# Probabilities turned one period later, beside the new scores, in a fused gated attention and FFN block

## The reference

```python
# x, ctx: (32, 64, 512); H, HKV, DK = 32, 8, 128
Q = (layernorm(x) @ Wq.T).reshape(b, s, 8, 4, 128)
K = (ctx @ Wk.T).reshape(b, s, 8, 128)
V = (ctx @ Wv.T).reshape(b, s, 8, 128)
scores = einsum('bqhed,bkhd->bheqk', Q, K) * 128 ** -0.5     # causal
attn = einsum('bheqk,bkhd->bqhed', softmax(scores), V)
x = x + tanh(g_xattn) * (attn @ Wd.T)
...
x = x + tanh(g_ffn) * down(silu(gate(layernorm(x))) * up(layernorm(x)))
# gate, up, down: weights w * (su @ sv), inner size 1792
```

## Time and the profile before

| | us |
|---|---|
| median of 3 runs | 1472.08 (1470.79 to 1472.47) |
| the profiled execution | 1472.51 |
| its span, first to last instruction | 1470.7 |
| TensorE matmuls busy | 1451.0 (99%) |
| VectorE busy | 1070.5 (73%) |
| GpSimd busy | 820.2 (56%) |
| ScalarE busy | 642.4 (44%) |
| TensorE idle before a matmul, the longest of them in attention | 1.1 |

### The profile page before, as it was taken

The page is one execution under the profiler, slowest core; times in us unless marked ns, Lnnn a source line. Parts: engine busy times, 40 slices in busy tenths (PEclk is TensorE's granted clock), DMA queues, the critical chain, the costliest instruction groups (busy, mean ns, idle before and its releaser), DMA issues.

```text
span 1470.7 us, 20673 instructions
## 1 busy us (share of the span) xinstructions
PE 1451.0 (99%) x7322; PEld 1185.7 (81%) x7322; DVE 1070.5 (73%) x1578; ACT 642.4 (44%) x1118; POOL 820.2 (56%) x727
## 2 busy tenths in 40 slices
PE   8999999999999999999999999999999999999998
PEld 8878788888888777777777777887888888888887
DVE  5366677877677777767777778777488878767676
ACT  5355454554444343343433444443444444333343
POOL 5598899998888212111111332233388877666664
PEclk9999999999999999999999999999999999999999
DMA  8476677778987644333433334332011121311112
GB/s 274 150 229 210 221 253 250 260 232 291 361 268 265 229 142 140 115 115 134 139 115 115 115 124 155 138 137 65 22 59 50 43 61 48 122 43 59 49 55 75
DMA packets 116070, 218.02 MB, mean 148 GB/s; under 512 B 9472, under 2 KB 47616, under 8 KB 113920
## 3 DMA queue, kind: packets, MB, share of 16 engines
q1 hardware_dynamic: 115968, 216.70, 44.0%
HBM read 151.13 MB, written 65.54 MB: 147 GB/s over the span
## 4 chain that ended last, share of the span: by engine, by line
PE 90%; DVE 5%; issue 1%; DMA 1%; POOL 1%; ACT 1%; SPq 0%; DVEq 0%; ACTq 0%; POOLq 0%
PE bank L543 66%; PE bank L709 4%; PE bank L662 4%; PE bank L845 3%; PE bank L844 3%; PE bank L846 3%; PE bank L671 2%; PE bank L689 2%; DVE el L1265 1%; PE bank L587 1%; DMA c_raw<-in_ctx_t 1%; DVE er L1265 1%; PE bank L742 1%; DVE xc L1259 0%; DMA w_raw<-in_w 0%
## 5 line engine op out<-in xcount | busy, mean ns | idle before, releaser
L1601 POOL TENSOR_TENSOR wd_lo<-wd_raw,wd_hi 128x512 fp32r<-128x512 f32 x64 | 81.9, 1302 | 370.6 <-ACT wd_hi L1011 370.6
L543 PE MATMUL bank<-xc,wa_hi 128*128 128x512 f32 x896 | 277.3, 391 | 0.0
L543 PE MATMUL bank<-wd_hi,o_hi 128*128 128x512 f32 x512 | 202.4, 395 | 0.0
L543 PE MATMUL bank<-wd_hi,o_lo 128*128 128x512 f32 x512 | 199.9, 390 | 0.0
L543 PE MATMUL bank<-wd_lo,o_hi 128*128 128x512 f32 x512 | 199.5, 390 | 0.0
L543 PEld LDWEIGHTS bank<-xc,wa_hi 128*128 128x128 f32 x896 | 167.8, 188 | 35.9 <-issue 1.1
L543 PE MATMUL bank<-xc,wa_lo 128*128 128x512 f32 x448 | 174.5, 390 | 0.0
L1352 DVE TENSOR_TENSOR o_lo<-bank,o_hi 128x512 fp32r<-128x512 f32 x128 | 82.0, 682 | 100.2 <-ACT o_hi L1042 100.2
L1429 DVE SCALAR_TENSOR_TENSOR X<-bank,tg,X 128x512 f32<-128x512 f32 x221 | 154.4, 741 | 0.0
L543 PE MATMUL bank<-x_hi,wf_hi 128*128 128x512 f32 x392 | 153.1, 391 | 0.0
L543 PE MATMUL bank<-x_hi,wf_lo 128*128 128x512 f32 x392 | 152.5, 389 | 0.0
(11 more groups left out here) (180 smaller groups left out, 3411.1 us busy)
## 6 DMA issues: line engine op xcount, KB each, us to landing
q_scratch<-q_st SPq DMA_DIRECT2D x32, 1024.0 KB, 4.3
q_sb<-q_scratch SPq DMA_DIRECT2D x64, 512.0 KB, 5.7
w_raw<-in_wq SPq DMA_DIRECT2D x32, 512.0 KB, 4.0
wd_raw<-in_wd SPq DMA_DIRECT2D x16, 1024.0 KB, 5.1
f_raw<-ffn_eff_scratch SPq DMA_DIRECT2D x28, 512.0 KB, 3.6
er_raw<-in_sf_r SPq DMA_DIRECT2D x42, 256.0 KB, 4.0
e_raw<-in_wf SPq DMA_DIRECT2D x42, 256.0 KB, 5.3
ffn_eff_scratch<-e_eff SPq DMA_DIRECT2D x42, 256.0 KB, 5.1
```

Of the source, the lines that this page charges most:

```text
L543: last = pe.matmul(to, a, b, start=(start and n == 0), stop=(stop and n == 3 * len(pairs) - 1), skip_group_check=onto)
L1601: g.tensor_tensor(wd_lo[h % 2][:, e, :], wd_raw[:, e, :], f32(wd_hi[h % 2][:, e, :]), ALU.subtract).then_inc(g_wd, 1)
```

## The change

TensorE's period becomes: scores of u and u+1, probability transpositions of u-2 and u-1, score transpositions of u and u+1, weighted values of u-2 and u-1, outputs. `prob` has four buffers instead of two. ScalarE copies the new scores before the turned probabilities, and splits output weights before `out_hi(u-1)`. VectorE takes `masked_minus_max(u)` before `out_lo(u-2)`, and one addition to X goes between the two normalisations. At the entry, unit 0's probabilities are turned in bank 4 and output (0, 1) goes to bank 4. At the exit, the last pair's probabilities are turned within the FFN's first step.

```diff
-    prob = [at(15, "prob0", [P, CB * G // 2, S]), at(203, "prob1", [P, CB * G // 2, S])]
+    prob = [at(kib, f"prob{n}", [P, CB * G // 2, S]) for n, kib in enumerate((15, 203, 199, 201))]
@@ output_bank(u, t) @@
-            return 6 if t else 1
+            return (6 if u else 4) if t else 1
...
     def prob_bank(u):
-        return 7 if u == 0 else 2 + u % 2
+        return 4 if u == 0 else 2 + u % 2
@@ TensorE, scores(u) @@
             if u == 3:
                 pe.wait_ge(v_e, NP)
-                pe.wait_ge(a_pt, 1)
             elif u:
                 pe.wait_ge(v_add, u if u < 3 else u - 1)
-            if u >= 4 and u % 2 == 0:
+            if u >= 6 and u % 2 == 0:
                 pe.wait_ge(v_y, 2 * u - 6)
@@ TensorE, prob_transposes(u) @@
             if u == 0:
-                pe.wait_ge(v_e, NP - 1)
+                pe.wait_ge(a_xt, 16)
@@ TensorE, weighted_values(u) @@
                 pe.wait_ge(v_o, 2 * u - 2)
+                if u == 2:
+                    pe.wait_ge(v_y, 2)
@@ TensorE, output(u, t), even u @@
-                else:
+                elif u:
                     pe.wait_ge(v_add, u + 3)
...
-        prob_transposes(1)
         for p in range(1, NPAIR):
             u = 2 * p
             scores(u)
             scores(u + 1)
             if p > 1:
+                prob_transposes(u - 2)
+            prob_transposes(u - 1)
+            score_transposes(u)
+            score_transposes(u + 1)
+            if p > 1:
                 weighted_values(u - 2)
             weighted_values(u - 1)
-            score_transposes(u)
-            score_transposes(u + 1)
             if p > 1:
                 output(u - 3, 1)
             output(u - 2, 0)
...
-            prob_transposes(u)
-            prob_transposes(u + 1)
...
             ffn_product(n, 1, 0, 0, 0)
+            if n == 0:
+                prob_transposes(NU - 2)
+                prob_transposes(NU - 1)
@@ ScalarE, scores_out(u) @@
-            else:
-                a.wait_ge(p_pt, u - 1)
+            elif u == 2:
+
+                a.wait_ge(v_c21, NQ)
+            elif u >= 4:
+                a.wait_ge(p_pt, u - 3)
@@ ScalarE, down_hi(n) @@
-            if 0 < n < NF - 1:
+            if n == 0:
+
+                a.wait_ge(p_pt, NU)
+            elif n < NF - 1:
                 a.wait_ge(p_yf, 8 * n)
@@ ScalarE, attention's loop (probs_out of the last pair moves into ffn(0)) @@
+            scores_out(u)
+            scores_out(u + 1)
             if p > 1:
                 probs_out(u - 2)
             probs_out(u - 1)
-            scores_out(u)
-            scores_out(u + 1)
             if p > 1:
                 out_hi(u - 2)
             exponentials(u)
-            out_hi(u - 1)
             if p in WD_STEP:
                 k, heads = WD_STEP[p]
                 for e in heads:
                     output_hi(k, e)
+            out_hi(u - 1)
             exponentials(u + 1)
@@ VectorE, attention's loop @@
+            masked_minus_max(u)
             if p > 1:
                 out_lo(u - 2)
-            masked_minus_max(u)
             masked_minus_max(u + 1)
             if p > 1:
                 add_to_x(u - 3, 1)
             out_lo(u - 1)
             normalised(u)
+            add_to_x(u - 2, 0)
             normalised(u + 1)
-            add_to_x(u - 2, 0)
             add_to_x(u - 2, 1)
             add_to_x(u - 1, 0)
```

More of the change, by code:

```diff
@@ L671, in score_transposes @@
                 last = pe.transpose(bank[score_bank(u)][:, n * P:(n + 1) * P],
-                                    prob[u % 2][:, 2 * n:2 * n + 2, :].rearrange("p b k -> p (b k)"), ident[:, :])
+                                    prob[u % 4][:, 2 * n:2 * n + 2, :].rearrange("p b k -> p (b k)"), ident[:, :])
             last.then_inc(p_s, 1)
@@ L689, in prob_transposes @@
                     last = pe.transpose(bank[prob_bank(u)][:, (2 * t + ep) * P:(2 * t + ep + 1) * P],
-                                        prob[u % 2][:, 4 * t + 2 * ep:4 * t + 2 * ep + 2, :].rearrange("p b k -> p (b k)"),
+                                        prob[u % 4][:, 4 * t + 2 * ep:4 * t + 2 * ep + 2, :].rearrange("p b k -> p (b k)"),
                                         ident[:, :])
@@ L1020, in scores_out @@
                 a.wait_ge(g_wa, 3 * NW)
-            else:
-                a.wait_ge(p_pt, u - 1)
-            a.activation(prob[u % 2][:, :, :].rearrange("p n k -> p (n k)"), bank[score_bank(u)][:, :],
+            elif u == 2:
+                a.wait_ge(v_c21, NQ)
+            elif u >= 4:
+                a.wait_ge(p_pt, u - 3)
+            a.activation(prob[u % 4][:, :, :].rearrange("p n k -> p (n k)"), bank[score_bank(u)][:, :],
                          ACT.Copy).then_inc(a_st, 1)
@@ L1027, in exponentials @@
             a.wait_ge(v_sub, u + 1)
-            a.activation(prob[u % 2][:, :, :], prob[u % 2][:, :, :], ACT.Exp, scale=SCALE).then_inc(a_exp, 1)
+            a.activation(prob[u % 4][:, :, :], prob[u % 4][:, :, :], ACT.Exp, scale=SCALE).then_inc(a_exp, 1)
         def probs_out(u):
@@ L1123, in ffn @@
             if n == 0:
+                probs_out(NU - 2)
+                probs_out(NU - 1)
                 out_hi(NU - 2)
@@ L1202, in _ @@
                     gate_up_hi(0, part)
-        probs_out(NU - 2)
-        probs_out(NU - 1)
         for n in range(NF):
@@ L1321, in masked_minus_max @@
             v.wait_ge(p_s, u + 1)
-            v.tensor_tensor(prob[u % 2][:, :, :], bank[score_bank(u)][:, :].rearrange("p (n k) -> p n k", k=S),
+            v.tensor_tensor(prob[u % 4][:, :, :], bank[score_bank(u)][:, :].rearrange("p (n k) -> p n k", k=S),
                             mask[:, :].rearrange("p (o k) -> p o k", o=1).broadcast_to(rows), ALU.add
@@ L1325, in masked_minus_max @@
             v.wait_ge(v_add, u + 1)
-            v.tensor_reduce(row_max[:, :], prob[u % 2][:, :, :], AX.X, ALU.max).then_inc(v_max, 1)
+            v.tensor_reduce(row_max[:, :], prob[u % 4][:, :, :], AX.X, ALU.max).then_inc(v_max, 1)
             v.wait_ge(v_max, u + 1)
-            v.tensor_tensor(prob[u % 2][:, :, :], prob[u % 2][:, :, :],
+            v.tensor_tensor(prob[u % 4][:, :, :], prob[u % 4][:, :, :],
                             row_max[:, :].rearrange("p (n o) -> p n o", o=1).broadcast_to(rows),
@@ L1333, in normalised @@
             v.wait_ge(a_exp, u + 1)
-            v.tensor_reduce(row_sum[:, :], prob[u % 2][:, :, :], AX.X, ALU.add).then_inc(v_sum, 1)
+            v.tensor_reduce(row_sum[:, :], prob[u % 4][:, :, :], AX.X, ALU.add).then_inc(v_sum, 1)
             v.wait_ge(v_sum, u + 1)
```

## The result

The changed kernel takes 1491.3 us (1490.52 to 1491.81) against 1472.2 us in the same measurement: ratio 1.0129, 95% interval 1.0117 to 1.0141. The forecast was 1490. Its profiled execution has a span of 1489.7 us, 19.0 more than before.

The account below looks back on a forecast made before the run. TensorE was taken as the bound, busy without waits in the steady periods. Shape changes +5.9, entry -2.7 and late load +15 gave +18 us, a median of 1490 us, range 1484 to 1499.

Parts of the forecast that it names:

- The period without a late load: Steady TensorE period: four tile-shape changes instead of three, 16.82 us instead of 16.63, +5.9 us over 31 periods.
- The entry: Attention's entry: TensorE's three waits go, 2.2 us in sum and 0.16 more each, -2.7 us.
- The late load: Every second period: output weights land at 10.4 us, so scores wait 1.13 us for VectorE's last addition; 15 us.
- The sum: Whole kernel: 5.9 - 2.7 + 15 = +18 us, a median of 1490 us; chance 0.84.
- Both halves of the mechanism: Periods with a load: weights issued later, behind the values, and ScalarE's copies placed behind the weight splits; 15 us.
- the first rival: Periods with a load: load not late or ScalarE's chain ends in time, only +3.2, 1475.3 us; chance 0.08.
- third rival: Waits of about 2 us lower TensorE's clock; +24, 1514 us if each of 14 waits did; chance 0.04.
- The second rival: TensorE's pipe hides shape changes by loading next weights during last matmuls; entry's gain stays, 1469.4 us; chance 0.04.

Follow-up runs that it names:

- the kernel with the entry alone: The kernel before with only the entry's banks, four buffers and later turning of unit 1, old order from period 2 on: 1468.9 us, ratio 0.9980.
- the kernel with the later load: The changed kernel with SyncE issuing the next output weights one step later, behind the next load of v: 1541.82 us, ratio 1.0473.
- the kernel with the copies first: The changed kernel with ScalarE's out_hi(u-1) copies put back ahead of the weight splits, the load still late: 1475.19 us, ratio 1.0017.
- the early load: The changed kernel with SyncE issuing the next output weights ahead of the load of v: 1474.27 us, and 1475.15 us when run once more.

## Why the prediction was right, point by point

**The period without a late load** was forecast at 16.82 and is 16.81. In the kernel after, scores take 1.88, the sixteen transpositions 1.90 (575.90 to 577.79), values 1.93, outputs 11.11. The transition that no row of before showed, scores into transpositions, cost what I took from values into transpositions. That it is the number of shape changes is shown by the kernel with five of them: 0.17 us each, with the same instructions and no wait.

**The entry** was forecast at -2.7. In the kernel with the entry alone it is -2.71 with one further shape change in it, which the forecast counted among the 31, so the waits gave 2.9 against 2.7.

**The late load** was forecast at 15 us and cost 16.2: twelve periods were 1.31 longer than 16.81 on average, the two with extra transpositions 0.2. The sum's terms: load at 5.31 (forecast 5.32); ScalarE's start at 10.20 to 11.04 in the period, 10.48 on average and 10.4 as median (forecast 10.2 to 11.3, 10.4 as median); from there to the scores 7.61 us (7.55). The signal from the addition to the scores took 0.15, not 0.10; over 14 periods that makes 0.7 of the missing 1.2 us.

**The sum** was 5.9 - 2.7 + 15 = 18; with what the runs showed it is 5.6 - 2.9 + 16.2 = 18.9, and the span grew by 19.0. The two smaller terms were a little too high and the larger one too low, so the total is off by 0.9 us where the load's term alone is off by 1.2. One reading beside the sum was wrong: before the change VectorE's second addition ended at 15.4 in the period (789.31 and 1.40 more), which leaves 1.2 us to the next scores and not 2.

**Both halves of the mechanism** are shown by the experiments: remove the lateness, or the copies' place behind the splits, or one normalisation from the chain, and 15 to 17 us go each time, down to 1474 to 1476. That is the 1475.3 of the first rival: it described the kernel that each of these small edits makes. The late load's slope, 1.0 us of period for each us of landing, is shown by the 14 odd periods of the changed kernel and by 10 of the 14 in the kernel with the later load.

**The clock** (third rival) stayed at 1.00 in waits of up to 1.5 us. In the kernel with the later load it did fall, in 12 of 14 waits of 2.0 to 4.1 us. So the rival named a real mechanism, and this change stayed clear of it. Its condition, a wait of about 2 us, is not borne out as it stands: waits of 2.7 and 3.1 us passed at full clock in that kernel, and the 1.9 us of idle TensorE near 66 us, on which the rival rested, are in all eleven traces, with a fall of the clock behind them in four (the kernel before is one) and none in seven (the changed kernel is one). **The second rival** is out: hiding the shape changes is not what TensorE did.

What remains of the change when its fault is mended is +2.2 to +2.9 us (1474.27 and 1475.15 against 1472.06 and 1472.3): the 31 shape changes at 0.18, 5.6, less the 2.9 of the entry gives 2.7.

## What to carry to other kernels

When a step is moved on the busiest engine, follow everything that is released by it, DMA queues above all: here the moved step gated one small load (128 KB of v), and behind it in the same queue stood a large one (1 MB) that had 0.2 us to spare. And when an engine's in-order program puts a wait for a DMA ahead of work that others need, the landing time goes straight into the period. A different order of the same matmuls has its own price, by the number of changes of tile shape; count those before looking at the waits.

## What the runs showed of the hardware

- One more change of tile shape in a period costs 0.17 to 0.18 us of TensorE's time: 0.35 for two in the kernel with five, 0.18 for one in the changed kernel. By the spacing of starts a single change costs from 0.14 (outputs to scores) to 0.2 us (values to outputs). This agrees with what the Trainium skill says of a drain when the tiling mode changes (TensorEngine Tiling (Array Packing), Key Properties).
- The 1 MB load of output weights took 4.9 to 6.0 us in the kernels before and after, where it was issued ahead of the loads of q and k (6.7 once in the kernel with the copies first), and 6.3 to 8.4 right behind them (median 7.1); with the early load, some 3 us behind a load of q and k of the period before, the median was 6.6. I had expected only its issue to move. That the loads share the DMA engines' time would explain it; no run separates that from the place in the queue.
- TensorE's granted clock went to its lower level, half of the higher one, in 12 of the 14 periods of the kernel with the later load that had a single wait of 2.0 to 4.1 us; these waits came back every 39 us or so. It stayed at the higher one in the two with waits of 2.7 and 3.1 us, and through waits of up to 1.5 us in every second period of the changed kernel. The length of a wait alone does not tell whether the clock falls.
- A multiplication of VectorE within `prob` (128x512, float32) takes 0.69 us, and 1.1 to 1.7 beside GpSimd's split of output weights, in the 14 odd periods of the kernel with the copies first.
- A loss of 0.33 us in every period can be missing from the waits of TensorE, since most of it lies within the modelled length of the matmul before. Only the spacing of starts shows it.
